# A four-stage vision kernel: the tails of two scan stages pipelined, and the local attention's step reordered

## Time and profile before

| | us |
|---|---|
| median of 3 runs | 18072.52 (18067.99 to 18101.30) |
| profiled execution, its own time | 18087.81 |
| its span in the profile | 18086.0 |
| tail of L1, each of two | 115 and 116 |
| L2, local attention | 962 |
| tail of L3: norm and gate, each of two | 84 and 84 |
| tail of L3: block, each of two | 307 and 308 |

### The profile page before, as it was taken

The page is one execution under the profiler, slowest core; times in us unless marked ns, Lnnn a source line. Parts: engine busy times, 40 slices in busy tenths (PEclk is TensorE's granted clock), DMA queues, the critical chain, the costliest instruction groups (busy, mean ns, idle before and its releaser), DMA issues. The chain is left out here.

```text
span 18086.0 us, 184332 instructions
## 1 busy us (share of the span) xinstructions
PE 14292.3 (79%) x38972; PEld 5918.2 (33%) x38972; DVE 15507.5 (86%) x20601; ACT 11827.0 (65%) x24107; POOL 12383.2 (68%) x5929
## 2 busy tenths in 40 slices
PE   7998878888888868888888868767777767777776
PEld 2222233333333323333333325423333233333333
DVE  6666489999999979999999964489999958999996
ACT  3555556667777636767677734378888827888882
POOL 0000079999999939999999941179988806998881
PEclk9999899999999989999999977788888888888888
DMA  1000033333333323333333321122222212222220
GB/s 27 13 18 11 12 93 107 106 107 107 107 107 106 102 77 106 108 106 107 107 106 107 106 78 37 37 67 81 82 79 79 78 29 72 81 81 79 79 80 29
DMA packets 542714, 1404.62 MB, mean 78 GB/s; under 512 B 135503, under 2 KB 191863, under 8 KB 538599
## 3 DMA queue, kind: packets, MB, share of 16 engines
q1 hardware_dynamic: 541586, 1392.84, 27.0%
HBM read 1311.24 MB, written 58.30 MB: 76 GB/s over the span
## 5 line engine op out<-in xcount | busy, mean ns | idle before, releaser
L996 PE MATMUL PS<-Hc,ident 128*128 128x448 f32 x16128 | 7494.1, 598 | 1950.8 <-POOL Hc L1308 1596.6
L1300 POOL TENSOR_TENSOR Tr<-du,BC 128x1344 f32<-128x1344 f32 x2688 | 8161.1, 3036 | 60.7 <-DVE du L1179 60.5
L996 PEld LDWEIGHTS PS<-Hc,ident 128*128 128x128 f32 x16128 | 3106.2, 205 | 6212.5 <-POOL Hc L1308 2579.3
L1118 ACT ACTIVATE PS<-dl,A 128x448 f32<-128x448 f32 x5376 | 3403.3, 633 | 2049.9 <-DVE Hr L1226 1248.6
L1308 POOL TENSOR_TENSOR Hc<-Hr,BC 128x448 f32<-128x448 f32 (+1 forms) x2688 | 3892.6, 1448 | 1030.1 <-DVE Hr L1226 947.2
L1226 DVE TENSOR_TENSOR_SCAN PS<-PS,st,Tr 128x448 f32<-128x448 f32 x3072 | 3358.2, 1135 | 142.8 <-ACT st L1132 140.6
L1233 DVE TENSOR_TENSOR Hc<-PS,BC 128x448 f32<-128x448 f32 x4480 | 2564.0, 605 | 0.0
L1126 ACT ACTIVATE PS<-cs,lneps,A 128x448 f32<-128x448 f32 x2688 | 1941.0, 722 | 175.2 <-DVE PS L1226 171.6
L719 POOL MEMSET pad<- 128x348 f32 x6 | 2.3, 387 | 2800.6 <-POOLq L67 2800.6
L1209 DVE SCALAR_TENSOR_TENSOR PS<-PS,Tr 128x448 f32<-128x448 f32 x2688 | 1644.2, 612 | 225.0 <-ACT PS L1126 214.0
L1118 ACT ACTIVATE Ar<-dl,A 128x448 f32<-128x448 f32 x2688 | 1765.5, 657 | 0.0
(11 more groups left out here) (254 smaller groups left out, 16125.1 us busy)
## 6 DMA issues: line engine op xcount, KB each, us to landing
BC<-bcscratch SPq DMA_DIRECT2D x5376, 224.0 KB, 3.6
zscratch<-zst SPq DMA_DIRECT2D x84, 224.0 KB, 2.0
bcscratch<-rows SPq DMA_DIRECT2D x336, 56.0 KB, 2.9
z<-zscratch SPq DMA_DIRECT2D x28, 672.0 KB, 4.5
xg<-mid SPq DMA_DIRECT2D x12, 1176.0 KB, 8.3
xr<-mid SPq DMA_DIRECT2D x56, 168.0 KB, 2.6
rl<-rows SPq DMA_DIRECT2D x56, 168.0 KB, 3.5
Q<-part SPq DMA_DIRECT2D x72, 98.0 KB, 4.4
```

Of the source, the lines that this page charges most:

```text
L996: e.matmul(PS[:, YB + c, 0:T], K["ident"][:], Hc[:, g % NHC, c, :], start=False, stop=(nn == 15)).then_inc(y_done, 1)
L1118: e.activation(decay_at(u), dl[:, q % 2, c, :], ACT.Exp, scale=A[:, q // NT, c, nn:nn + 1]).then_inc(a_done, 1)
L1300: e.tensor_tensor(Tr[:, g % NTR], du[:, q % 2], b, ALU.mult).then_inc(t_done, 1)
```

## The change

Part A, a new class `NormGate` in place of `TailNorm` and `Gate`. The chunks are summed on DVE (two adds), so the mean is one matmul; the squares are summed on POOL (two adds), and the variance comes out with pixels on partitions (four matmuls of two columns). Root and reciprocal are on 112x8 numbers; ACT widens the result (112x512), PE spreads it back with four matmuls of 112 columns. DVE scales from PSUM, ACT adds the bias, POOL multiplies by z.

Part B, `tail1` runs one loop of NT+3 rounds over all of this and the output products, with four banks for them.

Part C, `tail3` is one stage: norm, widening, taps, reduction of both images in one loop of rounds. Image two goes on without a pause; the taps of chunk 2 are on PE for 8 of the 14 tiles (`PE_TAPS`) and on DVE for 6; `t3` has room for both images; the closing multiply-add and store are in halves.

Part D, `local`: `add` stands at the head of DVE's step; `bias` behind the mask and a step later; the diagonal is gone, DVE scales the chosen weights by 1/sum (`scale`), and PE turns them by transposes; the two output products lie in two steps; small products are spaced wider and begin earlier; three banks (7, 5, 6) and three counts for image 0; bands, roots and scaling of the next image are earlier; the image is loaded ahead of the weights and two images ahead; POOL scales tiles 2 to 6 of image 0 within the steps.

```diff
+class NormGate:
...
+    def dve_sum(self, e, t):
...
+        e.tensor_tensor(s, self.y(0, t), self.y(1, t), ALU.add).then_inc(self.summed, 1)
+        e.wait_ge(self.summed, 2 * t + 1)
+        e.tensor_tensor(s, s, self.y(2, t), ALU.add).then_inc(self.summed, 1)
...
+    def pool_sum(self, e, t):
...
+        e.tensor_tensor(s, self.sq[:, t % 2, 0, :], self.sq[:, t % 2, 1, :], ALU.add).then_inc(self.sq_summed, 1)
+        e.wait_ge(self.sq_summed, 2 * t + 1)
+        e.tensor_tensor(s, s, self.sq[:, t % 2, 2, :], ALU.add).then_inc(self.sq_summed, 1)
...
+        for q in range(4):
+            a = e.matmul(self.PS[0:112, 6, 2 * q:2 * q + 2], self.sqsum[:, t % 2, 112 * q:112 * q + 112],
+                         self.K["blk"][:, 0:128:64], start=True, stop=True)
...
+        e.reciprocal(self.rs[:, t % 2, :], self.sd[:, t % 2, :]).then_inc(self.inverse, 1)
...
+        for q in range(4):
+            a = e.matmul(self.PS[:, 7, 112 * q:112 * q + 112], self.wide[:, t % 2, q, :], self.K["ident"][0:112, 0:112],
+                         start=True, stop=True)
...
+    def pool_gate(self, e, t):
...
+            a = e.tensor_tensor(self.y(c, t), self.y(c, t), rows8(self.z[:, t % 2, c, :]), ALU.mult)
...
 def tail1(chip, K, D, pair, src, dst, yacc, zd):
...
+            for r in range(NT + 3):
+                if r < NT:
+                    norm.pe_mean(e, r)
+                if 0 <= r - 1 < NT:
+                    norm.pe_var(e, r - 1)
+                if r >= 3:
+                    out(r - 3, 0)
+                if 0 <= r - 1 < NT:
+                    norm.pe_spread(e, r - 1)
+                if r >= 3:
+                    out(r - 3, 1)
...
+            for r in range(NT + 2):
+                if r >= 2:
+                    norm.act_shift(e, r - 2)
+                if r < NT:
+                    norm.act_square(e, r)
+                if 0 <= r - 1 < NT:
+                    norm.act_root(e, r - 1)
+                    norm.act_widen(e, r - 1)
...
+            for r in range(NT + 3):
+                if r + 1 < NT:
+                    norm.dve_sum(e, r + 1)
+                if r < NT:
+                    norm.dve_centre(e, r)
+                if 0 <= r - 1 < NT:
+                    norm.dve_inverse(e, r - 1)
+                if r >= 4:
+                    add(r - 4, 1)
+                if 0 <= r - 1 < NT:
+                    norm.dve_scale(e, r - 1)
+                if r >= 3:
+                    add(r - 3, 0)
...
+PE_TAPS = (0, 1, 2, 4, 6, 8, 11, 13)
...
 def tail3(chip, K, D, pair, src, dst, yacc, zd):
...
+            e.wait_ge(w_ld, 112)
+            for r in range(NK + 6):
+                if r < NT:
+                    norm.pe_mean(e, r)
+                if 0 <= r - 1 < NT:
+                    norm.pe_var(e, r - 1)
+                if 0 <= r - 3 < NK:
+                    expand(r - 3, 0)
+                if 0 <= r - 1 < NT:
+                    norm.pe_spread(e, r - 1)
+                if 0 <= r - 3 < NK:
+                    expand(r - 3, 1)
+                    expand(r - 3, 2)
+                if r - 5 in PE_TAPS:
+                    tap(r - 5)
...
+                if 0 <= r - 6 < NK:
+                    reduce_(r - 6)
...
+            for r in range(NK + 5):
+                if r + 1 < NT:
+                    norm.dve_sum(e, r + 1)
+                if r < NT:
+                    norm.dve_centre(e, r)
+                if 0 <= r - 1 < NT:
+                    norm.dve_inverse(e, r - 1)
...
+                if 0 <= r - 5 < NK:
+                    tap(r - 5, 0)
+                if 0 <= r - 1 < NT:
+                    norm.dve_scale(e, r - 1)
+                if 0 <= r - 5 < NK:
+                    tap(r - 5, 1)
+                    if r - 5 not in PE_TAPS:
+                        tap(r - 5, 2)
+                if r == NT + 9:
+                    final(0)
+            total(1)
+            final(1)
...
 def small_products(s):
 
-    a = {4: ("mean", 0), 5: ("var", 0)}.get(s)
-    if CENTRE <= s < CENTRE + NT:
-        a = ("centre", s - CENTRE)
-    b = ("stat", s - STAT) if STAT <= s < STAT + NT else None
-    c = ("turn", s - TURN) if TURN <= s < TURN + 6 else None
+    a = {1: ("mean", 0), 2: ("var", 0)}.get(s)
+    if spaced(s, 4, NT) is not None:
+        a = ("centre", spaced(s, 4, NT))
+    b = ("stat", spaced(s, 5, NT)) if spaced(s, 5, NT) is not None else None
+    c = ("turn", spaced(s, 4, 6)) if spaced(s, 4, 6) is not None else None
...
+            return {0: 7, 1: 5, 2: 6}[KINDS[name]] if b == 0 else 7
...
-                        a = e.matmul(PS[0:kn, 2 + h, 112 * k:112 * k + 112], E[:, n % 2, off:off + kn], dg[:, n % 2, :],
-                                     start=True, stop=True)
+                        a = e.transpose(PS[0:kn, 2 + h, 112 * k:112 * k + 112], E[:, n % 2, off:off + kn],
+                                        K["ident"][0:112, 0:112])
...
+            def scale(n):
+                s, nk = n % 2, size(n)
+                e.wait_ge(chosen, n + 1)
+                e.wait_ge(divided, n + 1)
+                e.tensor_scalar(E[:, s, 0:nk], E[:, s, 0:nk], den[:, s, 1:2], None, ALU.mult).then_inc(scaled, 1)
...
-            for r in range(STEPS + 13):
+            for r in range(STEPS + 14):
                 b, s = divmod(r, NTL)
                 more = b + 1 < NI
+                if 0 <= r - 4 < STEPS:
+                    add(r - 4)
                 if r < STEPS:
                     mask_(r)
+                if band_step(r, 10) is not None:
+                    bias(band_step(r, 10))
...
-                if 0 <= r - 4 < STEPS:
-                    add(r - 4)
+                if 0 <= r - 1 < STEPS:
+                    scale(r - 1)
+                if r < STEPS:
+                    replace(r)
...
-            for u in range(NT):
+            for u in range(2):
                 scale(0, u)
```

More of the change, by code:

```diff
@@ L1434 @@
[L1434 to L1456, removed]
+    def dve_sum(self, e, t):
+        s = rows8(self.ysum[:, t % 2, :])
+        if t >= 2:
+            e.wait_ge(self.mean_mm, t - 1)
+        e.tensor_tensor(s, self.y(0, t), self.y(1, t), ALU.add).then_inc(self.summed, 1)
+        e.wait_ge(self.summed, 2 * t + 1)
+        e.tensor_tensor(s, s, self.y(2, t), ALU.add).then_inc(self.summed, 1)
@@ new lines, in dve_scale, with act_shift @@
+    def dve_scale(self, e, t):
+        e.wait_ge(self.spread_mm, t + 1)
+        e.wait_ge(self.centred, t + 1)
+        for c in range(3):
+            y = self.y(c, t)
+            a = e.scalar_tensor_tensor(out=y, in0=y, scalar=self.lg[:, c:c + 1], in1=rows8(self.PS[:, 7, 0:T]),
+                                       op0=ALU.mult, op1=ALU.mult)
+        a.then_inc(self.scaled, 1)
+    def act_shift(self, e, t):
+        e.wait_ge(self.scaled, t + 1)
+        for c in range(3):
+            a = e.activation(self.y(c, t), self.y(c, t), ACT.Identity, bias=self.lb[:, c:c + 1])
+        a.then_inc(self.shifted, 1)
@@ new lines, in pe, with drain, relu @@
+            squeeze(1)
+            excite(1)
+        def act(e):
+            def drain(k, c):
+                t = k % NT
+                u = place[k, c]
+                if u == 0:
+                    e.wait_ge(pad_zero, 1)
+                    e.wait_ge(folds[0].step, 5)
+                if k >= NT:
+                    e.wait_ge(tapped, 9 * tap_groups(min(k - NT + 1, NT - 1)))
+                    e.wait_ge(relued, min(k - NT + 2, NT))
+                e.wait_ge(full, u + 1)
+                e.activation(pad[:, c, 1 + 8 * t:9 + 8 * t, 1:57], rows8(PS[:, u % 4, 0:T]), ACT.Relu,
+                             scale=bn1[:, 0, c:c + 1], bias=bn1[:, 1, c:c + 1]).then_inc(drained, 1)
+            def relu(k):
+                v = k % 2
+                if k == 0:
+                    e.wait_ge(folds[1].step, 5)
+                if k >= 2:
+                    e.wait_ge(red_mm, k - 1)
+                if k in PE_TAPS:
+                    u = place[k, "tap"]
@@ L1834, in local @@
                 if what:
-                    order[b, what] = len(order)
+                    kind = KINDS[what[0]]
+                    ahead[b, what] = list(counts)
+                    order[b, what] = counts[kind]
+                    counts[kind] += 1
     with ExitStack() as ctx:
@@ L1988, in pe @@
                     hidden(band_step(r, 7), 1)
-                if band_step(r, 8) is not None:
-                    output(band_step(r, 8))
+                for h in range(2):
+                    if band_step(r, 8 + h) is not None:
+                        output(band_step(r, 8 + h), h)
         def act(e):
```

626 lines of the change are left out of this document (329 added, 297 removed).

## The result

The changed kernel takes 17,535.3 us (median of 4 runs, 17,528.8 to 17,547.3) against 18,080.2 beside it (18,068.0 to 18,101.3): a ratio of 0.970, with 0.968 to 0.972 as its 95% interval. The profiled execution took 17,537.7 us, its span is 17,535.7; before it was 18,086.0. So 550.3 us of the span are to be found. In one run further down (the pause filled) one execution of five took 24,887.6 us at a granted clock of 0.63, and its ratio is taken from the other four.

The account below looks back on a forecast made before the run. It took a circle through DVE's add to bound L2, and engines waiting on each other the tails; gains of 51 + 167 + 27 + 227 = 472 us gave 17,600 us, range 17,490 to 17,780.

Parts of the forecast that it names:

- The circle through the add: In L2, similarities, DVE's whole step ending in its add, gather and next similarities wait on each other; 1.03 us waiting goes.
- The steps of L2: L2's loop: each step falls from 7.5 to 5.4 us as PE paces; 108 steps gain 227 us.
- g: TensorE's granted clock in L2's steps, taken as 0.80, between L2's 0.75 and 0.85 in the tail of L1.
- rival 1: TensorE's clock goes up wholly in L2: step 4.4 us, 335 us for the steps, 17,490 us in all; chance 0.12.
- The rule for transposes: L2's turn: transposes taken at half the cost; the skill's four times for float32 would make the sum 46 us lower.
- Ahead of step 0: L2 before its loop: three banks for small products gain 24 us, the image's earlier load 3, together 27.
- the early start of step 0: L2: starting after two scaled tiles instead of seven gives nothing, as the first gather waits for key blocks' transfers.
- Tails of L1: The two tails of L1: a chain over engines paces rounds of 9.7 us; 90 against 115.5 us, twice 25.5 gained.
- the 6 us of allowances: Tail of L1: 3 us added for matmuls at low clock and 3 for DVE and POOL hindering each other.
- Tails of L3: The two tails of L3: DVE bounds with 34 tap groups; 308 against 391.5 us, twice 83.5 gained.
- rival 4: DVE and POOL block each other in the tails, 14 and 13 us longer each: +54, 17,655 us; chance 0.07.
- a sign of error: Tap groups in the tail of L3 stretching beyond 6.5 us would show the forecast wrong.

Follow-up runs that it names:

- the pause filled: The kernel before, with one added matmul of unread output in each step of local attention: 17,999.9 us, ratio 0.9965.
- The short gate: The kernel after, with POOL multiplying by z only one row of eight of each tile in all four tails: 17,509.6 us.
- the turns: The kernel before, with ScalarE's diagonal gone, VectorE scaling the weights and TensorE turning them by transposes, the add in its old place: 18,230.0 us, ratio 1.009.

## Why the prediction was right, and where it was not

**The circle through the add** was the right mechanism; it is shown by undoing it and by doing it alone.

**The steps of L2** were under-sized (227 of 321.3), and the term that failed is g, "I take 0.80". It was 0.93. With 0.93 the prediction's own formula gives 4.07/0.93 + 0.3 = 4.68 us, which is what was measured. That accounts for (5.4 - 4.68) x 108 = 78 of the 94 us; the other 16 are the count, as I took 108 steps of 7.5 us and the stretch held 112 of 7.55. The bound of 1.0 (rival 1, 0.12) lay nearer than the value taken. I had placed g between 0.75 and the 0.85 of another stage, though the rows at hand had the same loop at both levels, and the reason for the low one, the pause, was about to be removed. The work of 4.07 us was right: the turn's busy time at full clock fell from 1.36 to 84.6 x 0.93/112 = 0.70 us a step, a saving of 0.66 against 0.68 forecast.

**The rule for transposes.** 272 ns for a record at 0.93, against 316 at 0.75 before with twice as many records, is a factor of two for the whole turn, not four (0.70 against 1.36 us a step at full clock). The Trainium skill (TensorE: Matmul & The Clock Gate, Terms) has four times for float32; in this kernel the measurement decides, and it says half.

**Ahead of step 0**, 27 us became 2.5. The small products and the load gave 17.7 (the first scaling starts at +61.6 instead of +79.4; forecast 27, as a round needs all three products at the low clock, 4.4 us, and not 3.0). The new wait of `total(1)` then took 15 of them. The failing step is the one on the early start of step 0: I let the first gather follow the first scaling by 36.5 us as before, held by the key blocks alone. It follows by 51.8, since the change puts `total` into step 0 and its load behind the key blocks' transfers, and I had not priced that pair.

**Tails of L1**: 90 each was 84.3 and 87.0. The round was right, (6408.55 - 6359.22)/5 = 9.9 us against 9.7; the first round took 3.7 instead of 9.7, since no scaling stands in it, and the end 28 instead of 22. So two errors of 6 us cancelled, by luck, and the 6 us of allowances were hardly needed.

**Tails of L3**: 308 was 312.8 and 315.0. VectorE bounds them, as forecast; the first tap came at +64.0 and not 58, because the first add of the loop waited until +12.3 for the seven small weights, and the first rounds took 10.0 to 11.0 us.

**VectorE and POOL in each other's way** (rival 4) is real. The short gate gave back 12 us of VectorE's time in a layer-3 tail, where 16 x 1.12 = 18 were priced, and about 5 of them reached the end. The Trainium skill (SBUF — State Buffer, SBUF: two separate sides) says that such instructions exclude each other; the eight taps that grow by 3.0 us beside a gate (3.3 us) and sums agree. I had given it 0.07 as a case of its own, and allowed for it in the forecast as well, so that it came true without moving the total as the rival said (+54).

**The total** missed by less than its largest term: the 94 us missed in the steps of L2 and the 12 in the other stretches and 9 in the tails of L1 were offset by 24 and 12 us too many ahead of step 0 and in the tails of L3. What is left is the 78 us between the forecast gain of 472 and the measured 550.

**What an observer would have seen** held in the main but for three things: the first gather, the step of 4.68 instead of 5.4, and tap groups of 9.9 us beside a gate, beyond the 6.5 that I had named as a sign of error.

## What to carry to other kernels

Look for the one instruction whose place in an in-order engine's list closes a circle over several engines, and try its move alone, before any work is made smaller; making one engine's work smaller by giving an instruction to the engine that it waits for can cost time, as the turns did. Price TensorE's clock as part of the wait: where a pause in every step goes, read the clock of the fullest stretches of the same loop (1.00 here) and put the value near it rather than in a cautious middle; it came out at 0.93 and 0.98. When a reduction or a sum moves ahead in an engine's list, find the transfer that it waits for and what is queued behind it.

## What the runs showed of the hardware

TensorE's granted clock went with its waiting, in six versions of one loop: 0.61 with 266 us of waiting for the add, 0.62 with 245, 0.75 with 115, 0.86 with 92 and the matmul put in, 0.93 with 13, 0.98 with 1.7. TensorE's work differs between the versions too, so the table is no rule for the pause alone. Unread matmuls of 0.76 us in nearly every step made a kernel 0.35% faster. And in L2 the clock rose from its lower level to its higher one 15 to 33 us after the first gather in five kernels with one and the same loop, and 7 and 35 us after it in the last two, all of them as busy there; what sets the moment is open.
